# Gate logits of a two-layer mixture-of-experts tower: one block of matmuls per pair of tasks, and one for all four

## What is computed

```python
def _ple_layer(x, W, b, Gw, Gb, Gsw=None, Gsb=None):
    xe = x[:, EXPERT_IN_IDX, :]
    eo = relu(einsum('bed,edh->beh', xe, W) + b)
    gates = softmax(einsum('btd,tdk->btk', x[:, :T, :], Gw) + Gb)
    task_out = einsum('btk,btkh->bth', gates, eo[:, SEL, :])
    if Gsw is None:
        return task_out
    gs = softmax(x[:, T, :] @ Gsw + Gsb)
    shared_out = einsum('be,beh->bh', gs, eo)
    return concatenate([task_out, shared_out[:, None, :]], axis=1)
z = _ple_layer(_ple_layer(e, W0, b0, G0w, G0b, Gs0w, Gs0b), W1, b1, G1w, G1b)
h = maximum(concatenate([z, dense_ctx]) @ W_top1 + b_top1, 0)
y = maximum(h @ W_top2 + b_top2, 0) @ W_top3
```

## Time and profile before

| what | value |
|---|---|
| median of 3 runs | 1988.87 us (1988.82 to 1988.96) |
| profiled execution, its own time | 1988.91 us |
| its span, first to last instruction | 1986.8 us |
| PE busy | 1978.6 us, 100% |
| DVE busy | 1380.4 us, 69% |
| ACT busy | 705.6 us, 36% |
| granted TensorE clock | 1.00 (2.4 GHz) |
| HBM traffic | 117 GB/s over the span |

### The profile page before, as it was taken

How to read it: one execution, slowest core, us unless ns; L and a number is a source line. 1 busy time by engine, 2 the same in 40 slices (tenths; PEclk the granted TensorE clock), 3 DMA queues, 4 the chain that set the end, 5 groups by cost and what they waited for, 6 DMA issues and landing times.

```text
span 1986.8 us, 25812 instructions
## 1 busy us (share of the span) xinstructions
PE 1978.6 (100%) x8914; PEld 1611.6 (81%) x8914; DVE 1380.4 (69%) x1447; ACT 705.6 (36%) x944; POOL 168.7 (8%) x152
## 2 busy tenths in 40 slices
PE   8999999999999999999999999999999999999999
PEld 7878778788878887878878778787888878878787
DVE  5488998896266756667555988898943667566664
ACT  3233333333333233332434333333333232433333
POOL 5630000000030002122033000000000000000000
PEclk9999999999999999999999999999999999999999
DMA  6553334333353334343344434343333333343331
GB/s 218 173 161 107 130 94 131 108 118 99 95 162 95 119 97 144 105 140 119 101 142 137 130 87 138 96 128 120 106 99 90 117 96 117 96 119 96 116 95 43
DMA packets 70029, 232.69 MB, mean 117 GB/s; under 512 B 10100, under 2 KB 12668, under 8 KB 69960
## 3 DMA queue, kind: packets, MB, share of 16 engines
q1 hardware_dynamic: 61688, 210.76, 34.8%
q0 software_dynamic: 7488, 20.98, 3.3%
q10 hardware_dynamic: 784, 0.10, 0.0%
HBM read 231.58 MB, written 0.23 MB: 117 GB/s over the span
## 4 chain that ended last, share of the span: by engine, by line
PE 99%; DMA 0%; POOL 0%; ACT 0%; issue 0%
PE main L346 30%; PE main L347 29%; PE main L348 29%; PE top L346 3%; PE top L348 3%; PE top L347 3%; PE gps L386 2%; DMA eo_sh<-in_tbl,idx 0%; PE top L456 0%; DMA idx<-in_ids 0%; POOL eo_sh L311 0%; ACT eo_b L743 0%; PE top L514 0%; PE top L499 0%; PE gps L499 0%
## 5 line engine op out<-in xcount | busy, mean ns | idle before, releaser
L346 PE MATMUL main<-act_hi,w_hi 128*128 128x512 f32 (+1 forms) x2576 | 1003.3, 389 | 0.0
L347 PE MATMUL main<-act_lo,w_hi 128*128 128x512 f32 (+1 forms) x2576 | 1001.0, 389 | 0.0
L348 PE MATMUL main<-act_hi,w_lo 128*128 128x512 f32 (+1 forms) x2576 | 1000.5, 388 | 0.0
L880 DVE TENSOR_TENSOR w_lo<-raw,w_hi 128x1024 fp32r<-128x1024 f32 (+1 forms) x356 | 433.1, 1217 | 545.6 <-ACT w_hi L576 514.5
L576 ACT ACTIVATE w_hi<-raw 128x1024 fp32r<-128x1024 f32 (+1 forms) x356 | 375.8, 1056 | 1172.8 <-PE main L348 1060.8
L346 PEld LDWEIGHTS main<-act_hi,w_hi 128*128 128x128 f32 x2576 | 483.6, 188 | 116.0 <-issue 16.4
L348 PEld LDWEIGHTS main<-act_hi,w_lo 128*128 128x128 f32 x2576 | 483.6, 188 | 100.0
L347 PEld LDWEIGHTS main<-act_lo,w_hi 128*128 128x128 f32 x2576 | 483.7, 188 | 99.1
L960 DVE TENSOR_TENSOR slots<-slots,prod 128x1024 f32<-128x1024 f32 (+2 forms) x202 | 245.1, 1213 | 6.0
L337 POOL DMA_INDIRECT slots<-in_tbl,idx x144 | 164.6, 1143 | 899.7 <-DVE act_lo L892 603.3
L954 DVE TENSOR_TENSOR prod<-eo_sh,gate_b 128x1024 f32<-128x1024 f32 x136 | 165.6, 1217 | 2.0 <-DVE slots L960 0.5
(11 more groups left out here) (67 smaller groups left out, 456.2 us busy)
## 6 DMA issues: line engine op xcount, KB each, us to landing
raw<-in_w SPq DMA_DIRECT2D x304, 512.0 KB
gate_b<-gates_dram SPq DMA_DIRECT2D x34, 512.0 KB
raw<-in_w_top SPq DMA_DIRECT2D x32, 512.0 KB
raw<-in_w_first SPq DMA_DIRECT2D x16, 512.0 KB
gate_b<-gates_dram SPq DMA_DIRECT2D x16, 256.0 KB
slots<-in_tbl,idx POOLq DMA_INDIRECT x144
gw<-in_g_w SPq DMA_DIRECT2D x16, 128.0 KB
raw<-in_w_top SPq DMA_DIRECT2D x4, 256.0 KB
```

Of the source, the lines that this page charges most:

```text
L346: nc.tensor.matmul(dst, lhs_hi, rhs_hi, start=start, stop=False)
L347: nc.tensor.matmul(dst, lhs_hi, rhs_lo, start=False, stop=False)
L348: return nc.tensor.matmul(dst, lhs_lo, rhs_hi, start=False, stop=stop)
L880: nc.vector.tensor_tensor(w_lo[0:parts, slot, 0:cols], raw[0:parts, rawslot, 0:cols], w_hi[0:parts, slot, 0:cols], ALU.subtract).then_inc( ...
```

## The change

The logits of T0 and T1 are computed together after unit 0 of T0, those of T2 and T3 after unit 0 of T2 (`duo_logits`: 16 matmuls; quarters 0 and 1 of the array hold the even and odd input strips of the first task, quarters 2 and 3 those of the second). The logits of L0 to L3 are computed together in SH after unit 7 (`task_logits`: 32 matmuls, quarter t holds task t). The stationaries are 4 columns wide, not 32. The shared logits of step A stay as they were. So there are 4 blocks a half, 8 in all. The softmax of a pair runs on 64 partitions, that of all four tasks on 128, and for the four there are no quarters to be added. T1, T3 and L0 to L3 have no softmax, no wait of ACT for logits and no store of rows; their gate loads remain. `gw` is loaded 4 times a half, not 9. The store of a pair is 64 rows of 2 KB, that of the four tasks 128 rows. SP issues the latter in L0, between units 6 and 7. PE's loop `others` is cut in two of three turns in SH. `keep` is 4 instead of 2 at the changes behind T0 and T2, and the kept operations run at j = 1 of T1 and T3, ahead of the `w_lo` of unit 3, where the gates had been. The transposes of the last looked-up table move, in the first half, from T1 (j = 13, 14) and T2 (j = 13, 14) to T1 (three at j = 2, one at j = 13). ACT's loop over T1 and T2 is unrolled.

```diff
+            def duo_logits(J, h, t):
+                pe.wait_ge(gw_in, J * 16 + 16)
+                pe.wait_ge(logit_evac, J)
+                pe.wait_ge(x_done, x_sets(h, t + 1))
+                for r in range(KT // 2):
+                    for c in range(QUADS):
+                        which, k = c // 2, 2 * r + c % 2
+                        mm = nc.tensor.matmul(as_subs(gps[0][c * QUAD:c * QUAD + NG, :]),
+                                              gw[:, k, which * NG:(which + 1) * NG], x_strip((t + which) * KT, k),
+                                              start=(r == 0), stop=(r == KT // 2 - 1))
+                mm.then_inc(logit_done, 1)
+
+            def task_logits(J, mixed):
+                pe.wait_ge(gw_in, J * 16 + 16)
+                pe.wait_ge(logit_evac, J)
+                pe.wait_ge(pair_done, mixed)
+                for k in range(KT):
+                    for t in range(T):
+                        mm = nc.tensor.matmul(gps[0][t * QUAD:t * QUAD + NG, :], gw[:, k, t * NG:(t + 1) * NG],
+                                              slots[:, t * KT + k, :], start=(k == 0), stop=(k == KT - 1))
+                mm.then_inc(logit_done, 1)
...
+                for part in ((0, 3), (3, 6)) if tasks else ((0, 6),):
+                    with pe.Fori(*part) as i:
+                        for c in range(2):
+                            expert(c, U + 2 + c + i * 2, E + 2 + c + i * 2)
+                    if tasks and not part[0]:
+                        task_logits(*tasks)
...
+            def tasks_gates(J, Pb):
+                turned_logits(J)
+                bias = gbias_tasks[:, None, :].broadcast_to([P, blocks, T])
+                after(link(nc.vector.tensor_tensor(lg_tasks[:, :, :], bias, parts[:, :, 0:NG], ALU.add)))
+                less_max(lg_tasks, mx_tasks, P, NG)
+                inv = inverse_sum(J, lg_tasks, mx_tasks, rs_tasks, P, NG)
+                dve.wait_ge(pair_done, Pb)
+                after(link(nc.vector.tensor_tensor(turned_tasks[:, :, 1:1 + NG], lg_tasks[:, :, :], inv, ALU.mult)))
+                nc.vector.transpose(rows_tasks, prod[:, 0, :]).then_inc(rows_rdy, 1)
...
                     if j == 1 and gates:
-                        shifted(*gates)
-                        gate_rows(*gates)
-                    if j == 2:
+                        gates()
+                    if j == (1 if plan and not gates else 2):
                         run(late)
+                    if j == TASKS_AT and tasks:
+                        tasks_gates(*tasks)
...
-                      1: {13: [(0, 3, 0)], 14: [(0, 3, 1)]},
-                      2: {13: [(0, 3, 2)], 14: [(0, 3, 3)]},
+                      1: {2: [(0, 3, 0), (0, 3, 1), (0, 3, 2)], 13: [(0, 3, 3)]},
...
                     return change(U + STEP, V + STEP // RAW, off, s0 + 2 + t, (t + 1) * KT, ops, shared=last, x=not last,
-                                  keep=2)
+                                  keep=2 if t % DUO else 4)
```

More of the change, by code:

```diff
@@ L103, in build @@
         mx, rs = (sb(name, [GCOL, blocks]) for name in ("mx", "rs"))
+        lg_tasks = sb("lg_tasks", [P, blocks, T])
+        mx_tasks, rs_tasks = (sb(name, [P, blocks]) for name in ("mx_tasks", "rs_tasks"))
+        turned_tasks = prod[:, 0, :].rearrange("p (c i) -> p c i", i=GCOL)
+        rows_tasks = prod[:, 1, :]
         warm = sb("warm", [P, 2])
@@ L249, in _, with gated_stream @@
             FOR_SHARED, FOR_L0, FOR_L1 = ((4, 6),), ((0, 2), (2, 4), (4, 6)), ((1, 2), (2, 4), (4, 5))
-            def gated_stream(src, first, U, off, Q, parts, Pb, g=None, more=None, start=0):
+            def gated_stream(src, first, U, off, Q, parts, Pb, J=None, task=None, rows=None, g=None, more=None, start=0):
                 early = STEP // 2 - 1
@@ L269, in _ @@
             for h in range(HALVES):
-                (first, base), gated, p0 = places(h), h * GATED, h * PAIRS
+                (first, base), jobs, p0, later = places(h), h * JOBS, h * PAIRS, h * 2 * T + T
                 if h == 0:
@@ L426, in first_two, with plain_step @@
                 strips(1, U + 1, range(3, KT))
-            def plain_step(U, E, S, between=None, dense_of=None, order=range(KT), by_strips=False, gate=None):
+            def plain_step(U, E, S, between=None, dense_of=None, order=range(KT), by_strips=False, gate=None, tasks=None):
                 if by_strips:
@@ L434, in plain_step, with others @@
                     if gate:
-                        logits(*gate)
+                        gate()
                     expert(1, U + 1, E + 1)
[L437 to L443, removed]
+                others(U, E, dense_of, tasks)
+            def others(U, E, dense_of=None, tasks=None):
+                for part in ((0, 3), (3, 6)) if tasks else ((0, 6),):
[4 more added lines that the diff above has]
+                        task_logits(*tasks)
                 expert(0, U + DENSE_HOST, E + DENSE_HOST, between=None if dense_of is None else dense_sums(dense_of))
@@ L458, in dense_sums, with gated_step @@
                 return emit
-            def gated_step(U, E, S, Q, x, then=None, order=range(KT)):
+            def gated_step(U, E, S, gate=None, then=None, order=range(KT)):
                 def emit(i, k):
@@ L464, in emit @@
                         then()
-                plain_step(U, E, S, between=emit if then else None, order=order, gate=(Q, x))
+                plain_step(U, E, S, between=emit if then else None, order=order, gate=gate)
             def tower(U, S, stop=False):
@@ L613, in step @@
                         gate_slot(*gates)
+                    if j == TASKS_AT and tasks is not None:
+                        gate_slot(tasks, lg_tasks[:, :, :])
                     if j == 2 and y_of is not None:
@@ L801, in _ @@
                 task0(0, y_of=h - 1 if h else None)
-                with act.Fori(1, T - 1) as t:
+                for t in range(1, T - 1):
                     task0(t)
@@ L915, in gate_rows @@
[L915 to L929 removed]
+                less_max(lg, mx, GCOL, NE)
@@ L1038, in run, with step @@
                     op()
-            def step(U, V, off, ops=None, gates=None, plan=None, late=(), x={}, dense_of=None):
+            def step(U, V, off, ops=None, gates=None, plan=None, late=(), x={}, dense_of=None, tasks=None):
                 queue = []
@@ L1185, in _ @@
                 U = u0 + U_SH1
-                step(U, U // RAW, off, late=left, dense_of=h)
+                step(U, U // RAW, off, late=left, dense_of=h, tasks=(j0 + JOBS - 1, p0 + 8 * (T + 1)))
                 U = u0 + U_T1
@@ L1200, in task1 @@
                     ops = gating("layer1", t, E + STEP + n * STEP, Q + 1 + n, h, Pb + 8 + n * 8)
-                    step(Ut, Vt, off, ops, (Q + 1 + n, NG, T + 2 + n), x=turns[h].get("L", {}) if last else {})
+                    step(Ut, Vt, off, ops, x=turns[h].get("L", {}) if last else {})
                     change(Ut + STEP, Vt + STEP // RAW, off, Sn + 1, (t - 1) * KT, ops)
```

204 lines of the change are left out of this document (120 added, 84 removed).

## The result

The changed kernel takes **1985.08 us** (median of 14 runs, 1984.06 to 1986.63) against 1989.2 us for the kernel before (14 runs beside them, 1988.82 to 1990.9): ratio 0.9979, 95% interval 0.9973 to 0.9986. The forecast was 1984.9 us in a range of 1983.9 to 1989.3, with 0.48 for faster by over 0.2% and 0.39 for the same. Against no change at all the gain is clear: the interval ends at 0.9986.

A forecast was written before the change was run, and what follows sets the result against it. PE, busy throughout, was taken to bound the kernel: 1988.91 us less ten fixed block prices of 0.40 us, 4.0 us, with no new waits on PE, gives 1984.9 us, in a range of 1983.9 to 1989.3.

The forecast's parts named there:

- The bound: Whole kernel: time is what PE streams plus losses between kinds of matmul; work taken from DVE or ACT is worth nothing.
- The term of the sum: PE's logit blocks fall from 18 to 8, saving ten fixed prices of 0.40 us, 4.0 us.
- bound the fixed price of a new block between 0.3 and 0.5 us: Six new logit blocks on PE: going in and out taken near 0.40 us, moving the sum by 0.6 either way.
- rival 4: More is gained: a shorter way in or out, 0.1 to 0.2 us on each of 6 blocks, 1984.0 us; 8%.
- The nearest row: Profile row of 8 one-column matmuls, 16 records in 0.55 us, taken to show narrow stationaries run side by side.
- Rounds: Logit blocks on PE: 76 rounds before and after, price of a round unchanged at 0.429 us.
- Rival 5: Logit matmuls don't run side by side: 82 us more, 2067 us; 3%.
- rival 2: The clock falls to 1.2 GHz in SH's block of logits: 24.6 us more, 2009.5 us; 5%.
- The margin in T1 and T3: DVE after the hand-over: `w_lo` of unit 2 has 1.2 us to spare, of unit 3 0.65 us; nothing holds PE.
- Early gates: T1 and T3: gates land at 212.1 instead of 217.4, DVE's 2.5 us wait goes, worth nothing in time.
- SP: Stores stay hidden: a pair's 1.5 to 2.9 us, the 256 KB one in L0 at most 3.9 us.
- The chances: Faster by over 0.2% 0.48, same 0.39, slower 0.13; forecast 70%, lying on the 0.2% line of 3.98 us.

The follow-up runs named there:

- DVE work put back: The changed kernel with six transposes of 32x512, result unused, added on DVE at j = 1 of L0 to L3; 1985.37 us.
- eight pieces: The changed kernel with PE's loop in SH written out and SH's logit block cut into eight pieces of two rounds; 1989.92 us.

## Why the prediction was right, and where it wasn't

**The bound.** Right. The time is what PE streams and what it loses between kinds of matmul. DVE's lighter load is worth nothing (DVE work put back).

**The term of the sum.** Right in kind and nearly in size: ten fixed prices of 0.40 us, 4.0, against 4.15 to 4.25 in the trace and 4.12 between the medians. The price goes with the number of blocks and not with their length (eight pieces, and 3.43 us for eight rounds; with 4 columns it is 0.34 us in blocks of two and four rounds and 0.36 in those of eight and sixteen, a difference that no run explains). The step that was mis-sized is "bound the fixed price of a new block between 0.3 and 0.5 us", centred on 0.40: it is 0.36, which is the small gain of rival 4, six times 0.04. The nearest row was taken to show only that one column streams alike, and nothing said of the way in. That the forecast and the median lie within 0.2 us has some luck in it: the gain was 0.1 us larger than forecast, and the kernel before, in the runs beside, 0.3 us slower than the median that the forecast started from.

**Rounds.** Right: narrow stationaries run side by side, 0.429 us a round. Rival 5 is out, and so is rival 2: the granted clock is 1.00 through both blocks of SH and behind them (the first is shown).

```profile
505.00:513.00 8.00, 8.00 (x70) 2.17 (x69) 1.23 (x1) 1.64 (x2) 0.00 (x0) 1.00 0.30 92
513.00:519.00 6.00, 6.00 (x28) 4.95 (x27) 0.00 (x0) 0.80 (x1) 0.00 (x0) 1.00 0.00 0
```

(Columns as in the earlier trace rows.)

**The margin in T1 and T3.** Right: 1.2 and 0.63 us against 1.2 and 0.65 (the prediction's own terms, added up without rounding on the way, give 0.57). With two operations fewer kept back, PE waits just where and as long as this sum says. So the kept operations are no gain, they are what the gain needs: with two fewer 5.8 us go.

**Early gates.** Wrong in its last sentence: "It is worth nothing in time, since PE doesn't wait for it." In a step without a block PE arrives 2.1 us earlier at every unit. With the kept operations behind unit 3's `w_lo` the gates come too late for unit 5 in three of the four steps, 1.5 us, and the operations themselves too late for unit 4 in the other, 1.35 us. I had set the saved wait of DVE against the kernel before, where it was free, and not against the changed one, where it is used up. That this cost nothing was luck: the change had the early place, and the prediction saw no use in it. "No wait of DVE for gates in T1 and T3" was not quite so either. The kernel before had six waits for gates, two each in T1, T2 and T3, 17.2 us together; three are left that the view lists, two of 1.1 us in T2 and one of 0.3 us in T3:

```profile
DVE prod L1043 <- DMA gate_b<-tasks_dram: 2.5, 3, 1.1
```

**SP.** The stores are hidden, as said. The one of 256 KB was under-priced: it holds the queue for 570.28 - 565.94 = 4.34 us (4.27 in the second half), where 3.9 was the upper bound. It held nothing up: PE has no wait there.

```profile
565.94 0.42 SPq L244 DMA_DIRECT2D tasks_dram<-prod  x1
570.28 0.80 SPq L252 DMA_DIRECT2D gate_b<-tasks_dram  x2
```

**The chances.** That the forecast lay on the 0.2% line was seen, and the result can't be told from the line.

## What to carry to other kernels

When one engine is full, count how often it changes the way it works: here each excursion of TensorE to matmuls that use the array another way, and back, cost 0.34 to 0.47 us, however little was done in it. So put such matmuls together; or pad them to the full array where the padding is cheaper, as it was for the dense input. Removing work from the full engine makes every other engine's deadline earlier by as much; the gain is real only if the operations ahead of those deadlines are moved too, and that part is where to look for the margin. An order of work that is free in one version is not free in the next.

## What the runs showed of the hardware that was not expected

- A wait of PE costs more than its length: in the kernel with keep = 2, 1.18 us of waiting made a step 1.46 us longer, 0.28 us on top.
- The width of a stationary counts in the way in and out, though it doesn't in the rounds after the first: 0.40 us with 32 columns, 0.34 with 4, in a block of four rounds.
- The start varies more than all the rest. Two executions of the changed kernel had working distances within 0.1 us, and their first 128x512 matmuls 1.7 us apart. Of the fourteen traces six show the granted clock at its lower level, 1.2 GHz, in a stretch between 10.0 and 14.2 us; their first 128x512 matmul starts at 24.0 to 24.3 us. In six the clock is at its upper level, 2.4 GHz, from its first reading on, and that matmul starts at 22.6 to 23.3 us; two have no reading (23.5 and 23.8). PE's first wait, for the identity matrix, is 3.2 to 3.9 us long in both groups. Its waits for the looked-up rows, between 7 and 10.6 us, add up to 1.75 to 2.38 us in the six traces ahead of the lower clock, and to 0.77 to 1.66 in the six without it. The same stretch of the changed kernel in its own trace and in the second one (columns of the earlier trace rows; these waits were 1.75 us in the first and 1.00 in the second):

```profile
10.90:14.30 3.40, 3.40 (x19) 3.40 (x18) 2.48 (x4) 2.07 (x4) 0.95 (x1) 0.52 0.92 307
```

```profile
10.90:14.30 3.40, 2.93 (x26) 2.94 (x27) 2.42 (x5) 2.00 (x5) 1.17 (x2) 1.00 0.90 312
```

Which of these executions comes about doesn't go with what the kernels change, as far as fourteen traces tell. It goes with those waits, but no run varied them, so what decides it isn't shown.
